# Cross attention with int8-style rounding in a twelve-stage decoder kernel: rounding, value spreading and late steps moved between GpSimd, VectorE and ScalarE

## The reference, cut to what matters

```python
def _qdq(x):
    s = jnp.maximum(jnp.max(jnp.abs(x), axis=-1, keepdims=True) / 127.0, 1e-08)
    return jnp.clip(jnp.round(x / s), -127.0, 127.0) * s
q = _qdq(x) @ _qdq(wq).T + bq
kv = cond @ wkv.T + bkv
k, v = jnp.split(kv, 2, axis=-1)
...  # heads
attn = jax.nn.softmax(jnp.einsum('bnhd,bmhd->bhnm', q, k) * scale, axis=-1)
o = jnp.einsum('bhnm,bmhd->bnhd', attn, v).reshape(B, N, C)
out = _qdq(o) @ _qdq(wp).T + bp
x = _layernorm(x + out)
```

## Time and profile before

| | us |
|---|---|
| median of 3 runs | 4399.04 (4395.26 to 4401.97) |
| the profiled execution | 4387.83, its span 4386.0 |
| TensorE, VectorE, ScalarE, GpSimd busy | 3718.4, 3137.1, 1978.2, 1077.6 |
| cross attention, from 1582.6 to 1872.3 in the span | 289.7 |

### The profile page before, as it was taken

The page is one execution under the profiler, slowest core; times in us unless marked ns, Lnnn a source line. Parts: engine busy times, 40 slices in busy tenths (PEclk is TensorE's granted clock), DMA queues, the critical chain, the costliest instruction groups (busy, mean ns, idle before and its releaser), DMA issues. The chain is left out here.

```text
span 4386.0 us, 69593 instructions
## 1 busy us (share of the span) xinstructions
PE 3718.4 (85%) x25068; PEld 2253.6 (51%) x25068; DVE 3137.1 (72%) x7052; ACT 1978.2 (45%) x4709; POOL 1077.6 (25%) x1320
## 2 busy tenths in 40 slices
PE   7799999998833868698999989669999999997985
PEld 3466666665622446444555555444555555554543
DVE  7788989896577655333555568657888888886678
ACT  4466666665411423211333334225656555563345
POOL 2433321263010034200111122022323333232220
PEclk9899999999966979798999989879999999998797
DMA  2222222222101000020000000300000000001000
GB/s 66 69 66 64 68 53 69 60 63 54 53 29 33 1 22 2 1 71 21 1 1 1 1 30 2 120 0 1 1 1 1 1 1 1 1 1 46 1 2 20
DMA packets 220852, 120.23 MB, mean 27 GB/s; under 512 B 115296, under 2 KB 213344, under 8 KB 219296
## 3 DMA queue, kind: packets, MB, share of 16 engines
q1 hardware_dynamic: 220512, 115.78, 9.5%
HBM read 101.03 MB, written 14.68 MB: 26 GB/s over the span
## 5 line engine op out<-in xcount | busy, mean ns | idle before, releaser
L301 PE MATMUL ps<-xT,min 128*128 128x512 f32 (+1 forms) x1072 | 532.8, 626 | 7.7 <-DVE mZ L3180 5.4
L3185 DVE SCALAR_TENSOR_TENSOR macc<-ps,mcw,macc 128x508 f32<-128x508 f32 (+2 forms) x408 | 302.9, 742 | 143.9 <-ACT macc L3109 134.4
L3123 ACT ACTIVATE mE<-ps,mcol 128x128 f32<-128x128 f32 x1024 | 290.5, 369 | 7.5 <-PE ps L3025 0.4
L3271 POOL TENSOR_TENSOR mE<-mE,mCB 128x512 f32<-128x512 f32 x128 | 163.6, 1278 | 479.9 <-ACT mE L3123 479.9
L301 PEld LDWEIGHTS ps<-xT,min 128*128 128x128 f32 (+1 forms) x1072 | 182.4, 190 | 190.7 <-issue 179.9
L3055 PE MATMUL ps<-mwo,macc 128*128 128x256 f32 x1024 | 245.9, 383 | 19.2 <-DVE macc L3219 19.2
L2617 ACT ACTIVATE hE<-ps 128x512 f32<-128x512 f32 x256 | 138.9, 595 | 219.9 <-PE ps L2579 219.9
L3278 POOL TENSOR_TENSOR mSQ<-mSQ,mtn 128x512 f32<-128x512 f32 x128 | 163.5, 1277 | 255.9 <-ACT mtn L3127 255.9
L2152 ACT ACTIVATE lP<-ps,lm 128x128 f32<-128x128 f32 x256 | 90.4, 365 | 266.4 <-DVE lm L2212 266.4
L3055 PEld LDWEIGHTS ps<-mwo,macc 128*128 128x128 f32 x1024 | 185.8, 191 | 47.3 <-DVE macc L3219 25.7
L2243 POOL TENSOR_TENSOR lP<-lP,lm 128x512 f32<-128x512 f32 x64 | 66.5, 1040 | 575.4 <-DVE lm L2216 575.4
(11 more groups left out here) (594 smaller groups left out, 9108.2 us busy)
## 6 DMA issues: line engine op xcount, KB each, us to landing
dwk<-in_L_attn_Wk SPq DMA_DIRECT2D x64, 128.0 KB, 2.3
dwq<-in_L_attn_Wq SPq DMA_DIRECT2D x64, 128.0 KB, 2.3
dwv<-in_L_attn_Wv SPq DMA_DIRECT2D x64, 128.0 KB, 2.4
dwg<-in_L_attn_Wg SPq DMA_DIRECT2D x64, 128.0 KB, 2.4
dwo<-in_L_attn_Wo SPq DMA_DIRECT2D x64, 128.0 KB, 2.7
min<-in_m_in SPq DMA_DIRECT2D x2, 4096.0 KB, 17.6
d_N<-dNT SPq DMA_DIRECT2D x256, 16.0 KB, 1.5
dTT<-d_TT SPq DMA_DIRECT2D x256, 16.0 KB, 1.9
```

The costliest lines, as they stand in the source:

```text
L301: t = pe.matmul(out, w[:, j, :], self.c.xT[:, j, blk(g, 512)], start=j == 0, stop=j == 1)
L3123: x = act.activation(self.E[s][:, e, blk(j)], bank(4 + e)[:, blk(j)], ACT.Exp, bias=self.col[:, 4 * g + j, 0, 2 * i + e:2 * i + e + 1])
L3185: x = dve.scalar_tensor_tensor(out=acc[:, :, 3 - j:T], in0=p[:, :, 0:T - 3 + j], scalar=self.cw[:, i, j:j + 1], in1=acc[:, :, 3 - j:T], op ...
L3271: pool.tensor_tensor(g4(self.E[s][:, 0, :]), g4(self.E[s][:, 0, :]), self.CB[g % 2][:, :, :], ALU.mult).then_inc(*self.m0.up)
```

## The change

- `rounded` runs on VectorE, directly behind `scales`, for weights and X.
- `oq` no longer multiplies by the step. VectorE clips the values with MAGIC still in them, in one instruction; ScalarE takes MAGIC away while it copies the transposed output (`keep_rows` with a bias of -MAGIC); the step comes in behind the output projection, as the scalar of a multiply-add with X (`sum`). The bias `bp` is added to the four rows in one further instruction.
- `v`: VectorE adds bias and bank directly into the even or odd heads of `VE`, two instructions for each half group; GpSimd only zeroes both `VE` buffers at the stage's start. ScalarE's copy, `V`, `rp` and its load are gone.
- Late steps: `wo` on VectorE becomes `sum`, `stats` and `scale`, at the ends of three iterations. For groups 0 to 2 `oq` stands at the end of 4g+5, `ot` in 4g+6, `wo` and `sum` in 4g+7, `stats` in 4g+10, `scale` in 4g+11, `turn` in 4g+12. For the last group: `oq` 17, `ot` 18, `wo` and `sum` 19, `stats` 20, `scale` 21, `turn` 22. `xq` is written at the end of an iteration and no longer at the start of the next; on VectorE's queue that is the same place.

```diff
@@ order
-            late = (("oq",), ("ot",), ("wo",), ("turn",))[k] if 0 <= g < 4 else ()
-            if t % 4 == 1 and t < 12:
-                yield "xq", t // 4 + 1, 0
+        mid = (("ot", 6, 6), ("wo", 7, 7), ("turn", 12, 10))
+        late = (("oq", 5, 5), ("scale", 11, 9), ("sum", 7, 7), ("stats", 10, 8))
...
+            if t < 12 and t % 4 == 0:
+                yield "xq", t // 4 + 1, 0
@@ rounded, keep_rows
-    def rounded(self, pool, own, x, s):
+    def rounded(self, dve, own, x, s, last):
         n = x.shape[1]
-        pool.wait_ge(own.sem, own(pool.tensor_scalar(x, x, MAGIC, 127.0, ALU.subtract, ALU.min)))
+        dve.wait_ge(own.sem, own(last))
+        dve.wait_ge(own.sem, own(dve.tensor_scalar(x, x, MAGIC, 127.0, ALU.subtract, ALU.min)))
         for j in range(n):
-            q = pool.tensor_scalar(x[:, j, :], x[:, j, :], -127.0, s[:, n + j:n + j + 1], ALU.max, ALU.mult)
+            q = dve.tensor_scalar(x[:, j, :], x[:, j, :], -127.0, s[:, n + j:n + j + 1], ALU.max, ALU.mult)
-            act.copy(out[:, :, blk(h, 256)].rearrange("p i (j t) -> p i j t", j=2),
+            act.activation(out[:, :, blk(h, 256)].rearrange("p i (j t) -> p i j t", j=2),
...
@@ tensor
-                room[k] = self.vk.at(2 * g + k + 1)
+                room[k] = self.ve.at(2 * g + k + 1)
-                    pe.wait_ge(*self.ve.at(g + 1))
+                    pe.wait_ge(*self.ve.at(2 * g + 2))
@@ vector
+            elif step == "v":
+                dve.wait_ge(*self.vp.at(2 * g + k + 1))
...
+                for e in range(2):
+                    x = dve.tensor_tensor(pairs(self.VE[gs][:, blk(k, 2), e, :])[:, :, :, e, :],
+                                          pairs(bank(k).rearrange("p (b f) -> p b f", b=2))[:, :, :, e, :],
+                                          pairs(bc(self.bv[:, :], 2))[:, :, :, e, :], ALU.add)
+                x.then_inc(*self.ve.up)
             elif step == "oq":
...
+                dve.wait_ge(own.sem, own(self.scales(dve, own, O, O, self.q12[1])))
+                dve.tensor_scalar(O, O, MAGIC + 127.0, MAGIC - 127.0, ALU.min, ALU.max).then_inc(*self.oq.up)
+            elif step == "sum":
...
                 for x in range(4):
-                    a = dve.tensor_tensor(c.R[:, x, :], bank(2 + x // 2)[:, blk(x % 2, 256)], self.XB[:, x, :], ALU.add)
+                    a = dve.scalar_tensor_tensor(out=c.R[:, x, :], in0=bank(2 + x // 2)[:, blk(x % 2, 256)], scalar=self.q12[1][:, 4 + x:5 + x],
+                                                 in1=c.X[:, 4 * g + x, :], op0=ALU.mult, op1=ALU.add)
                 a.then_inc(*self.sum.up)
                 dve.wait_ge(*self.sum.at(g + 1))
-                c.norm_vector(dve, own, self.n, g, [0] * 4)
+                biased = own(dve.tensor_tensor(c.R[:, :, :], c.R[:, :, :], bc(self.bp[:, :], 4), ALU.add))
+            elif step == "stats":
+                dve.wait_ge(own.sem, biased)
+                last = c.moments(dve, own, [(c.R[:, x, :], 0) for x in range(4)], c.st, c.rsq, 1e-5)
+            elif step == "scale":
+                dve.wait_ge(own.sem, last)
+                c.scale_vector(dve, g, c.R)
@@ gpsimd
-        for step, u, k in self.order():
...
+        for V in self.VE:
+            x = pool.memset(V[:, :, :, :], 0.0)
+        x.then_inc(*self.vz.up)
```

More of the change, by code:

```diff
@@ L1491, in order @@
                 yield x
-        for t in range(NB + 9):
+        mid = (("ot", 6, 6), ("wo", 7, 7), ("turn", 12, 10))
+        late = (("oq", 5, 5), ("scale", 11, 9), ("sum", 7, 7), ("stats", 10, 8))
+        for t in range(NB + 7):
             a, b = shared(t // 4 + 1)[t % 4] if t < 12 else (None, None)
-            g, k = divmod(t - 6, 4)
-            late = (("oq",), ("ot",), ("wo",), ("turn",))[k] if 0 <= g < 4 else ()
-            if t % 4 == 1 and t < 12:
-                yield "xq", t // 4 + 1, 0
-            for step, u, n in (("t", t - 1, 0), ("s", t, 0), ("o", t - 2, 0), ("t", t - 1, 1), ("o", t - 2, 1), ("a", 0, 0), ("sh", t, 0), ("b", 0, 0),
-                               ("y", t - 2, 0)):
+            for step, u, n in (("t", t - 1, 0), ("s", t, 0), ("o", t - 2, 0), ("t", t - 1, 1), ("o", t - 2, 1), ("mid", 0, 0), ("a", 0, 0), ("sh", t, 0),
+                               ("b", 0, 0), ("y", t - 2, 0), ("late", 0, 0)):
                 if step in ("a", "b"):
@@ L1503, in order @@
                         yield part
+                elif step in ("mid", "late"):
+                    for x, k, last in mid if step == "mid" else late:
+                        for g in range(4):
+                            if t == 4 * g + (last if g == 3 else k):
+                                yield x, g, 0
                 elif 0 <= u < NB:
                     yield step, u, n
[L1506 to L1510, removed]
+            if t < 12 and t % 4 == 0:
+                yield "xq", t // 4 + 1, 0
     def scales(self, dve, own, out, x, s):
@@ L1540, in turn_rows, with keep_rows @@
             room[banks[h]] = kept.at(n + h + 1)
[L1542 removed]
+    def keep_rows(self, act, out, done, kept, n, banks, bias=0.0):
         for h in range(2):
             act.wait_ge(*done.at(n + h + 1))
[L1545 to L1546 removed]
+            act.activation(out[:, :, blk(h, 256)].rearrange("p i (j t) -> p i j t", j=2),
+                           self.c.bank(banks[h]).rearrange("p (j i t) -> p i j t", j=2, i=2), ACT.Identity, bias=bias).then_inc(*kept.up)
     def tensor(self, pe):
@@ L1729, in vector @@
             if step == "w0":
-                self.scales(dve, own, self.wr[:, :, :], self.wr[:, :, :], self.ws).then_inc(*self.wa.up)
+                dve.memset(self.mg[:, :], -MAGIC)
                 for e in range(2):
@@ L1743, in vector @@
                 x.then_inc(*self.ready.up)
+                last = self.scales(dve, own, self.wr[:, :, :], self.wr[:, :, :], self.ws)
+                self.rounded(dve, own, self.wr[:, :, :], self.ws, last).then_inc(*self.wq.up)
             elif step == "xq":
@@ L1747, in vector @@
                     dve.wait_ge(*self.xtr.at(2 * g))
-                self.scales(dve, own, self.XA[:, :, :], c.X[:, blk(g, 4), :], self.q12[0]).then_inc(*self.xa.up)
+                last = self.scales(dve, own, self.XA[:, :, :], c.X[:, blk(g, 4), :], self.q12[0])
+                self.rounded(dve, own, self.XA[:, :, :], self.q12[0], last).then_inc(*self.xq.up)
+            elif step == "v":
+                dve.wait_ge(*self.vp.at(2 * g + k + 1))
+                if g == 0 and k == 0:
+                    dve.wait_ge(*self.vz.at(1))
+                if g >= 2:
+                    dve.wait_ge(*self.o.at(4 * g - 4))
+                pairs = lambda a: a.rearrange("p b (h e d) -> p b h e d", e=2, d=16)
+                for e in range(2):
[3 more added lines that the diff above has]
+                x.then_inc(*self.ve.up)
             elif step == "s":
@@ L1775, in vector @@
             elif step == "oq":
+                O = self.O[gs][:, :, :]
                 dve.wait_ge(*self.on.at(4 * g + 4))
-                self.scales(dve, own, self.O[gs][:, :, :], self.O[gs][:, :, :], self.q12[1]).then_inc(*self.oa.up)
-            elif step == "wo":
+                if g:
+                    dve.wait_ge(*self.sum.at(g))
+                dve.wait_ge(own.sem, own(self.scales(dve, own, O, O, self.q12[1])))
+                dve.tensor_scalar(O, O, MAGIC + 127.0, MAGIC - 127.0, ALU.min, ALU.max).then_inc(*self.oq.up)
+            elif step == "sum":
```

56 lines of the change are left out of this document (13 added, 43 removed).

## The result

| | before | after |
|---|---|---|
| median of 3 runs | 4399.04 (4395.26 to 4401.97) | 4351.08 (4350.02 to 4359.19) |
| the profiled execution, its span | 4387.83, 4386.0 | 4350.02, 4348.2 |
| cross attention | 289.7 | 242.2 |
| VectorE, GpSimd busy | 3137.1, 1077.6 | 3160.9, 966.3 |

The account below looks back on a forecast made before the run. Rounding on GpSimd was taken to stand on TensorE's path in cross attention, with waiting and a low clock after it. 9.0 - 0.5 + 34.4 + 12.3 - 10 = 45 us off 4399 gave 4354, range 4336 to 4376.

Parts of the forecast that it names:

- iterations 3 to 17: Middle of the cross attention stage, to the last `o`: from 193.0 to 158.7 us, 34.4 less, before 10 for the clock.
- the tail: From the last `o` to the stage's end: 22.2 us in place of 34.55, 12.3 less.
- The rule L - 1.7: VectorE work of length L put behind `y` stalls TensorE by L - 1.7 us, the rest being slack.
- 9.0 less 0.5: Stage start: first scores 9.0 us earlier by rounding on VectorE and faster `q`, less 0.5 for the first group's `v.1`.
- Up to iteration 3 I leave the rest as it was: Between first scores and iteration 3: no further gain, as `xq1` stands under TensorE's slow `k1` and `t`.
- The walk: Iteration-by-iteration sum for 3 to 17 at 2.4 GHz: 120.9 base, 15.0 late TensorE steps, 22.75 new stalls, 158.7 us.
- four falls of 3.2 us, a quarter hidden: Clock term over eight pauses of 1.9 to 2.6 us: 13 us lost, 10 us to give back; bounds 0 and 25.
- The second rival: The clock falls behind most pauses: 25 us given back instead of 10, 4369 us; chance 0.2.
- 7.95: In the tail, `ot3` and `wo3` take as long as before, 7.95 us at 1.2 GHz.
- Additions in full: Rival: from iteration 3 on VectorE's additions are paid in full, 40 us in place of 22.75, 4371 us; chance 0.06.
- A bound VectorE: Rival: VectorE becomes the stage's bound, busy 146 of some 245 us, slower than before at about 4410 us; chance 0.03.

Follow-up runs that it names:

- the old order: The changed kernel with oq, ot, wo, sum, stats, scale and turn at the places of the kernel before: 4350.08 us, ratio 0.9916, the stage 245.25 us.

## Why the prediction was right, and where not

The forecast was 45 us and 4354; the medians gave 48 and 4351.08, the stage 47.5. By part: up to iteration 3 12.4 for 8.5, iterations 3 to 17 23.5 for 24.4, the tail 11.4 for 12.3. So the mechanism was right; that the total is within 3 us is in part luck, as one miss of 3.9 us and two of 0.9 lie in opposite directions.

- **GpSimd was on the path, and its place was taken by VectorE's maxima.** Right, though GpSimd was on it with more than the rounding (see below). `rounded` at 1.9 us measured 0.69 + 1.14; the clip 0.69; four multiply-adds from a bank 1.66 for 1.6; the bias 1.22 for 1.23; `v` 0.76 for 0.85. The rule L - 1.7 was tested by the doubled clip and held at 0.72 for 0.69.
- **The start.** 9.0 less 0.5 was under-sized: scores 9.8 earlier, iteration 3 12.4 earlier. The step that failed is "Up to iteration 3 I leave the rest as it was", which was to give back 0.5 us and gained 2.6: in the changed kernel between the first scores and iteration 3 the clock was low for 6.8 us where it had been for 17.0, so `k1` and `t` there were not as slow as before.
- **Iterations 3 to 17.** The walk gave 158.7 at 2.4 GHz and 10 for the clock, 168.7; it was 169.5. By iteration, predicted and measured: 3: 9.3, 9.3; 5: 12.1, 12.1; 7: 12.6, 12.7; 9: 12.1, 12.1; 13: 7.0, 7.0, where the clock stood. And 11: 15.3, 15.1; 14: 9.9, 9.7. Where it fell: 6: 14.0, 15.4; 8: 10.9, 14.0; 10: 14.0, 15.6; 12: 11.1, 14.2; 15: 13.0, 14.5. Iterations over the walk sum to 10.8. The waits were 2.13 for 1.95 (5, 9), 2.11 for 2.5 and 0.89 to 0.98 for 0.9 (6, 10), 1.48 for 0.95 (8), 2.32 for 2.6 (11, 15), 2.97 for 2.4 (12), 1.77 for 1.9 (14).
- **The clock.** I took four falls of 3.2 us, a quarter hidden. There were four stretches of 6.8 us and one of 3.4, 15.3 us lost at half of their length, 10.8 paid. Which pause is followed by a fall I could not say, and no run settled it: 1.48 was, 1.65, 1.77 and 2.32 were not, and one and the same pause of 2.13 us in iteration 5 was passed at 1.00 in the changed kernel and followed by 3.4 low us with the values as before. So length alone doesn't decide. The second rival, falls behind most pauses, was nearer in count (5 of 9) than in price. The Trainium skill ("TensorE: Matmul & The Clock Gate", section "A second HAM failure mode: psum-queue depth-cycling") has repeated short idles make the clock go back and forth: the five fit that; four here without a fall, and four short ones of the old order, speak against it as a rule for every pause.
- **The tail.** 22.2 predicted, 23.1 measured: `ot3` to `sum3` took 8.95 instead of 7.95. I had read the 7.95 as all at 1.2 GHz, but in the kernel before the clock was back at 2.4 GHz from 1863.1, inside `wo3`, which took 5.26 us; in the changed kernel nearly all of `wo3` ran at the low level and took 6.17.
- **The rivals.** Additions in full did not come: most of VectorE's new work lay in slack (that rival's terms add up to 38.8 and not 40, which changes nothing). A bound VectorE did not come either; it was busy 139 us of 242.
- **What the sum didn't have.** The reasons held where I had walked them, but the sum gave no price for the spreading of the late steps by itself. It is worth 3 us and not the 15 to 22 that I then expected.
- **A reading that was wrong.** The prediction says of GpSimd's value spreading that it is not on the path. In the trace of before it is, in groups 0 and 1, which the rows of group 2 don't show. The timeline at `oq0`:

```profile
1684.28 5.72 POOL L1807 TENSOR_TENSOR xVE<-xV,crp 128x256 f32<-128x256 f32 x8
...
1685.28 2.78 DVE L1520 TENSOR_SCALAR xO<-xO,xq 128x256 f32<-128x256 f32 x4
...
1690.09 3.63 POOL L1526 TENSOR_SCALAR xO<-xO 128x1024 f32<-128x1024 f32 x1
```

Beside the eight products VectorE's multiply-adds took 2.78 us instead of 1.14, and GpSimd began to round only at 1690.09, when its products were done, 2.0 us after VectorE's hand-over at 1688.06. Together that is 3.6 us, just what `ot` waited longer in groups 0 and 1 (10.41) than in group 2 (6.77). The sum lost nothing by it, since the walk was built from the new order and not from these waits. With only the rounding moved, the same contention is the main part of the 8.7 us by which the stage missed its 33.

What stays open is what decides behind which pause the clock falls. TensorE's other work between pauses wasn't varied.

## What to carry to other kernels

When an engine that hands over late is replaced by a busier one, walk its queue: the next wait is on whatever stands behind the new work there, and its size is that work less the slack, one for one. Several waits of 2 us can cost more clock than one of 9 (here nine short ones 30.6 us at the low level, a 5.7 and a 9.2 together 17.0), so cut late work until each piece fits its slack, rather than spread it in pieces that each leave a wait. Before work goes from GpSimd to VectorE, look at what GpSimd still does beside it.

## What the runs showed of the hardware

- Beside GpSimd's reads of SBUF, 128x4 instructions of VectorE took 0.57 to 0.72 us in place of 0.16, nearly all of them in one run and every second one in another; rounding's multiplies took 4.03 in place of 1.14. Beside GpSimd's zeroing, `TENSOR_SCALAR` 128x4 with one input took 0.97, instructions with two inputs 0.16, moments (`bn`) 1.39 as alone.
- The granted clock fell to 1.2 GHz behind a pause of 1.48 us and not behind one of 2.32, in the same stage; a pause of 1.67 was followed by 10.2 us at the low level, one of 9.24 by 10.2 too.
